# Layer norms of a float32 Perceiver-like stack: second-half squares on VectorE, later feature tiles in pairs, one set of zero products less

## What is computed

```python
def _layernorm(x, axis=-1, eps=1e-05):
    m = jnp.mean(x, axis=axis, keepdims=True)
    v = jnp.var(x, axis=axis, keepdims=True)
    return (x - m) / jnp.sqrt(v + eps)
...
x = x + _L0_xattn_ref(_layernorm(x, axis=-1), ...)
x = x + _L0_attn_ref(_layernorm(x, axis=-1), ...)
x = x + _L0_ffn_ref(_layernorm(x, axis=-1), ...)
x = x + _L1_xattn_ref(_layernorm(x, axis=-1), ...)
x = x + _L1_attn_ref(_layernorm(x, axis=-1), ...)
x = x + _L1_ffn_ref(_layernorm(x, axis=-1), ...)
```

## Time and profile before

| what | value |
|---|---|
| median of 3 runs | 1405.85 us (1403.39, 1405.93, 1405.85) |
| profiled execution, its own time | 1405.07 us |
| its span, first to last instruction | 1403.2 us |
| PE busy | 1354.3 us, 97% of the span |
| DVE, ACT, POOL busy | 983.2, 629.8, 682.5 us (70%, 45%, 49%) |
| granted TensorE clock, mean | 0.994 |
| DMA, mean | 61 GB/s |

### The profile page before, as it was taken

The page is one execution under the profiler, slowest core; times in us unless marked ns, Lnnn a source line. Parts: engine busy times, 40 slices in busy tenths (PEclk is TensorE's granted clock), DMA queues, the critical chain, the costliest instruction groups (busy, mean ns, idle before and its releaser), DMA issues.

```text
span 1403.2 us, 23741 instructions
## 1 busy us (share of the span) xinstructions
PE 1354.3 (97%) x8774; PEld 1124.2 (80%) x8774; DVE 983.2 (70%) x1501; ACT 629.8 (45%) x1325; POOL 682.5 (49%) x473
## 2 busy tenths in 40 slices
PE   6999999999999998899999999999999999999998
PEld 4677778778877776899899899999778887767886
DVE  5456676668569998787777787877546777955555
ACT  3534443253343334666566666666325545431000
POOL 3342577678737774441341331500474655626663
PEclk9999999999999999999999999999999999999999
DMA  4121123323232221000000001000132221212231
GB/s 146 49 74 47 61 84 97 90 76 95 78 141 84 87 81 60 1 26 25 1 25 24 1 25 35 19 2 1 58 107 60 76 76 61 91 38 83 91 101 63
DMA packets 30892, 85.63 MB, mean 61 GB/s; under 512 B 3408, under 2 KB 3536, under 8 KB 30544
## 3 DMA queue, kind: packets, MB, share of 16 engines
q1 hardware_dynamic: 30800, 84.43, 19.2%
HBM read 83.37 MB, written 1.05 MB: 60 GB/s over the span
## 4 chain that ended last, share of the span: by engine, by line
PE 76%; DVE 10%; ACT 7%; issue 6%; POOL 0%; DMA 0%; DVEq 0%; ACTq 0%; POOLq 0%
PE psum L904 22%; PE psum L905 21%; PE psum L906 21%; PE psum L1442 3%; DVE part_max L2596 3%; ACT expo L1981 2%; PE psum L932 1%; PE psum L940 1%; ACT expo_t L1988 1%; ACT expo L1976 1%; DVE sq_sum L2826 1%; DVE expo_t L2174 1%; DVE q_pair L2174 1%; PE psum L1635 1%; PE psum L1622 1%
## 5 line engine op out<-in xcount | busy, mean ns | idle before, releaser
L660 POOL TENSOR_SCALAR wpair<-landing 128x1024 fp32r<-128x1024 f32 (+3 forms) x116 | 108.2, 933 | 386.0 <-PE psum L906 258.7
L663 POOL TENSOR_TENSOR wpair<-landing,wpair 128x1024 fp32r<-128x1024 f32 (+3 forms) x116 | 239.3, 2063 | 9.7
L904 PE MATMUL psum<-xn,wpair 128*128 128x512 f32 (+1 forms) x552 | 212.3, 385 | 1.2 <-POOL wpair L663 0.8
L905 PE MATMUL psum<-xn,wpair 128*128 128x512 f32 (+1 forms) x552 | 208.1, 377 | 0.0
L906 PE MATMUL psum<-xn,wpair 128*128 128x512 f32 (+1 forms) x552 | 207.5, 376 | 0.0
L2174 DVE TENSOR_TENSOR expo_t<-psum,expo_t 128x512 fp32r<-128x512 f32 (+1 forms) x224 | 143.5, 651 | 76.7 <-ACT expo_t L1988 69.2
L1988 ACT CAST expo_t<-psum 128x512 fp32r<-128x512 f32 (+1 forms) x224 | 124.3, 565 | 123.8 <-PE psum L1442 123.8
L904 PE MATMUL psum<-expo_t,kv_pair 128*128 128x256 f32 (+1 forms) x416 | 133.7, 321 | 0.2 <-DVE expo_t L2174 0.2
L1442 PE MATMUL psum<-const,expo 128*128 128x128 f32 (+1 forms) x832 | 128.1, 273 | 5.3 <-DVE expo_t L2174 4.6
L2596 DVE TENSOR_REDUCE part_max<-psum 128x1 f32<-128x804 f32 x126 | 121.3, 988 | 6.1 <-PE psum L906 2.1
L761 POOL TENSOR_TENSOR wpair<-landing,wpair 128x512 fp32r<-128x512 f32 x80 | 120.9, 1511 | 6.7
(11 more groups left out here) (326 smaller groups left out, 3285.3 us busy)
## 6 DMA issues: line engine op xcount, KB each, us to landing
landing<-in_weights SPq DMA_DIRECT2D x75, 512.0 KB, 3.6
landing<-in_weights SPq DMA_DIRECT2D x105, 256.0 KB, 2.6
kv<-in_ctx SPq DMA_DIRECT2D x8, 832.0 KB, 4.4
landing<-in_weights SPq DMA_DIRECT2D x15, 320.0 KB, 2.8
rope_k<-in_rope_k SPq DMA_DIRECT2D x1, 1664.0 KB, 7.7
const<-in_constants SPq DMA_DIRECT2D x1, 1184.0 KB, 8.7
x<-in_x SPq DMA_DIRECT2D x4, 256.0 KB, 4.2
out<-x SPq DMA_DIRECT2D x1, 1024.0 KB, 4.3
```

The costliest lines, as they stand in the source:

```text
L660: pool.tensor_scalar(wpair[:, slot, 0, 0:width], landing[:, slot, 0:width], 1.0, 1.0, ALU.mult, ALU.mult).then_inc(chunk_high, 1)
L663: pool.tensor_tensor(wpair[:, slot, 1, 0:width], landing[:, slot, 0:width], wpair[:, slot, 0, 0:width].bitcast(F32), ALU.subtract).then_in ...
L904: pe.matmul(out, w(0), act(0), start=start, stop=False)
L905: pe.matmul(out, w(0), act(1), start=False, stop=False)
```

## The change

In layer norms 1 to 5 the squares of half 1 are made by DVE (`late_squares`), right behind the four subtractions, and counted on a semaphore of their own; ACT makes those of half 0 only. PE leaves out the six zero products between the two sets of square sums. In all six layer norms the normalisation works in five groups in place of eight single tiles: half 0 as tile 0, tile 1, tiles 2 and 3 together; half 1 as tiles 0 and 1 together, tiles 2 and 3 together. Product with 1/deviation, high part and low part are one instruction for a group. On ACT, Ln and Exp of half 1 now come behind the second high part instead of the fourth; on DVE, the product with 1/deviation runs two groups ahead of the low part. PE's `normal_ready` waits for the group that holds its tile.

```diff
+        NORMAL_GROUPS = ((0, 0, 1), (0, 1, 2), (0, 2, 4), (1, 0, 2), (1, 2, 4))
...
             def square_sums(k, half, pair):
 
-                pe.wait_ge(ln_squared, 4 * k + 2 * half + pair + 1)
+                if half and k:
+                    pe.wait_ge(ln_squared_late, 2 * (k - 1) + pair + 1)
+                else:
+                    pe.wait_ge(ln_squared, 2 * k + 2 * min(k, 1) + 2 * half + pair + 1)
...
                 for half in range(2):
-                    if k:
-                        keep_going(LN_BANKS[k][1 + half], 6)
+                    if k and not half:
+                        keep_going(LN_BANKS[k][1], 6)
...
             def normal_ready(k, half, f):
-                pe.wait_ge(ln_low, 8 * k + 4 * half + f + 1)
+                pe.wait_ge(ln_low, 5 * k + (((1, 2, 3, 3), (4, 4, 5, 5))[half][f]))
...
-                def high(half, f):
-                    act.wait_ge(ln_normal, 8 * k + 4 * half + f + 1)
-                    act.copy(xn[:, 0, f, HALVES[half]], xc[:, f, HALVES[half]]).then_inc(ln_high, 1)
+                def high(group):
+                    half, first, end = NORMAL_GROUPS[group]
+                    act.wait_ge(ln_normal, 5 * k + group + 1)
+                    act.copy(xn[:, 0, first:end, HALVES[half]], xc[:, first:end, HALVES[half]]).then_inc(ln_high, 1)
...
                 deviation(0)
-                squares(1, 0)
-                high(0, 0)
-                squares(1, 1)
-                for f in range(1, FT):
-                    high(0, f)
+                if not k:
+                    squares(1, 0)
+                high(0)
+                if not k:
+                    squares(1, 1)
+                high(1)
                 deviation(1)
-                for f in range(FT):
-                    high(1, f)
+                for group in (2, 3, 4):
+                    high(group)
...
-                def normalise(half):
+                def late_squares():
+                    dve.wait_ge(ln_centred, 4 * k + 4)
+                    for pair in range(2):
+                        tiles = xc[:, 2 * pair:2 * pair + 2, HALVES[1]]
+                        dve.tensor_tensor(sq[:, 2 * pair:2 * pair + 2, HALVES[1]], tiles, tiles, ALU.mult
+                                          ).then_inc(ln_squared_late, 1)
+
+                def normalise(group):
+                    half, first, end = NORMAL_GROUPS[group]
                     cols = HALVES[half]
                     dve.wait_ge(ln_rstd, 2 * k + half + 1)
-                    for f in range(FT + 1):
-                        if f < FT:
-                            dve.tensor_tensor(xc[:, f, cols], xc[:, f, cols], rstd[:, cols], ALU.mult).then_inc(ln_normal, 1)
-                        if f:
-                            dve.wait_ge(ln_high, 8 * k + 4 * half + f)
-                            low(xn[:, 1, f - 1, cols], xc[:, f - 1, cols], xn[:, 0, f - 1, cols]).then_inc(ln_low, 1)
+                    tiles = xc[:, first:end, cols]
+                    dve.tensor_tensor(tiles, tiles, rstd[:, cols].unsqueeze(1).broadcast_to([P, end - first, T // 2]),
+                                      ALU.mult).then_inc(ln_normal, 1)
+
+                def normal_low(group):
+                    half, first, end = NORMAL_GROUPS[group]
+                    dve.wait_ge(ln_high, 5 * k + group + 1)
+                    low(xn[:, 1, first:end, HALVES[half]], xc[:, first:end, HALVES[half]],
+                        xn[:, 0, first:end, HALVES[half]]).then_inc(ln_low, 1)
 
                 dve.wait_ge(ln_mean, k + 1)
                 centre(0)
                 centre(1)
+                if k:
+                    late_squares()
                 if meanwhile is not None:
                     meanwhile()
                 normalise(0)
                 normalise(1)
+                for group in range(5):
+                    normal_low(group)
+                    if group < 3:
+                        normalise(group + 2)
```

More of the change, by code:

```diff
@@ L462, in perceiver_stack @@
         ln_high, ln_low = sem("ln_high"), sem("ln_low")
+        ln_squared_late = sem("ln_squared_late")
         stored = sem("stored")
```

## The result

| | before | change |
|---|---|---|
| median of the runs taken together | 1405.89 us (6 runs, 1403.39 to 1408.46) | 1399.12 us (6 runs, 1394.86 to 1400.91) |
| ratio to before, 95% interval | | 0.9949, 0.9934 to 0.9963 |
| profiled execution, span | 1405.07, 1403.2 us | 1399.93, 1397.7 us |
| granted clock of the profiled execution | 0.994 | 0.996 |
| DVE instructions executed | 1501 | 1475 |

A second set of 10 runs of the same kernel gave 1400.59 us, just inside the range, and over all 16 the median is 1399.88.

The account below looks back on a forecast made before the run. PE was taken to bound the kernel behind each layer norm. Savings of 0.41 (layer norm 0), 0.69 (1, 3, 4) and 1.88 (2, 5) sum to 2.98 us, taking 1405.07 to 1402.1; range 1400.0 to 1404.9.

Parts of the forecast that it names:

- PE is thus 0.9 us late because ACT does the squares: Layer norm 1: first product starts at 76.83 though its low part was ready at 75.93; the change starts it 0.85 earlier.
- so they cost DVE nothing: Layer norm 1: DVE's two squares end near 73.43 and 74.03, while DVE was idle until 74.61.
- the overlap of 0.08 between DVE's instructions: Layer norms: each DVE instruction starts before the last ends; without this overlap the saving would be 1.57 us in all.
- the sums by place: Savings: 0.41 us in layer norm 0, 0.23 each in 1, 3 and 4, 0.94 each in 2 and 5.
- Here the order costs something: Layer norm 1: half 1's multiplication precedes a low part PE needs; new waits of 0.13 and 0.38, 0.62 of 0.85 lost.
- The gain does not arrive: Rival: a later meeting point, such as a PE wait for POOL, does not move; time stays near 1405; chance 0.12.
- Slower, by POOL: Rival: POOL's weight splits stretch DVE's new squares by up to 0.84 in layer norm 2; 1408 us; chance 0.04.
- DVE issues 16 instructions in place of 20 ... that is worth nothing more.: Layer norms 1 to 5: fewer DVE and ACT instructions save no further time, as both finish before PE.
- a way to be slower: Rival: PE's new layer norm gaps drop the clock to 1.2 GHz; one fall gives 1407.9, all five 1436; chance 0.03.

Follow-up runs that it names:

- before_ten_more: Kernel before with ten more DVE instructions at its start (the memset of zero_b cut into eleven pieces): median 1398.34 us, ratio 0.9952.
- change_36_more: Changed kernel with 36 more DVE instructions at its start: median 1395.98 us, ratio 0.9931 to before.
- before_ten_more_filled: Kernel before with ten more DVE instructions at its start and zero products ahead of three PE waits in stages D and E: 1397.38 us, ratio 0.9938.
- change_36_more_filled: Changed kernel with 36 more DVE instructions at its start and zero products ahead of three PE waits in stages D and E: 1391.43 us, ratio 0.9902.
- pairs_only: Changed kernel with ACT's squares of half 1 and both sets of zero products put back, tiles still in five groups: 1407.84 us, ratio 1.0020 to before.

## Why the prediction was too small, point by point

- *"PE is thus 0.9 us late because ACT does the squares"*: right. The first product is 0.75 earlier (0.85 forecast), and with squares_only, which moves the squares and drops the zero products but makes no pairs, the layer norms are as short as with the whole change.
- *"so they cost DVE nothing"*, and the overlap of 0.08 between DVE's instructions: right, as were the sums by place: 0.23 and 0.23, 0.94 against 0.87 and 0.95, 0.41 against 0.43. The rule of the Trainium skill's page "VectorE: DVE Perf Modes", section "The DRAIN you can't avoid", would have made it 1.57; the trace sides with its exception.
- *"Here the order costs something"*: right in kind, 0.23 in place of 0.38 of waiting ahead of the third tile. It costs nothing in all, since PE's first start was 0.1 later than reckoned. But the pairs also bring nothing: in layer norm 1 single tiles end at 12.25, the pairs within 0.1 of that. Their share in layer norms 1 to 5 is about zero; in layer norm 0 they are the whole of the 0.43.
- *"The gain does not arrive"*, *"Slower, by POOL"*: neither came about, and POOL's stretching was 0.27.
- **The step that failed: "DVE issues 16 instructions in place of 20 ... that is worth nothing more."** What it was worth is not the instructions' time but their number. A loop moved 18 instructions forward in DVE's stream, and at its two jumps back PE then waited 1.26 in place of 1.95 us, which is 1.4 us of waits and, by the length of stage D, 1.0 of time. The rows for it stood in the trace before (5.4 us of DVE waiting for "issue" in the stretch 660 to 830, all in two waits) and weren't read, because only the layer norms were. The Trainium skill's page "Runtime: NRT & Kernel Launch", section "Instruction fetch mechanics", says that a taken branch whose target isn't in what was fetched forces a new fetch. The idle times of 2.65 and 2.75 at the jump back, and their going with ten memsets and with some ten instruction packets fewer (28 in place of 38), agree. That the instructions had to be fetched anew is thus the likely reason, but it wasn't seen directly: the runs show that the stall hangs on how many instructions stand ahead of the loop. None of them gives a rule for its size.
- **The second step: the clock.** The sum was set against one execution at 0.994, and the clock came in only as a way to be slower, with the earlier trace rows against it. Three things were amiss. That window's 1.00 said little (in another execution of the same kernel the clock fell in layer norm 0, at 18.9, where that window ends). Outside the layer norms the clock already fell three times, for 6.8 us. And it could rise: with the shorter wait at the jump back it went from 0.9936 to 0.9957, some 2.5 us at 1.2 per 0.001. The Trainium skill's page "TensorE: Matmul & The Clock Gate", section "What's actually happening", has the clock halved after idle time; in these runs most falls, 23 of 30, stood beside a wait of PE of 1.8 to 2.4 us, but such a wait did not bring one every time, and five came with no wait at all. By that page of the Trainium skill the gaps that the change opens in the layer norms (0.60 and 0.23 us) were a reason to fear for it; the window 72 to 78 after shows 1.00:

```profile
72.00:78.00 6.00, 5.17 (x28) 3.96 (x26) 5.25 (x11) 3.62 (x9) 0.15 (x1) 1.00 0.31 87
```

In sum 2.94 (forecast 2.98) + 1.0 to 1.4 + some 2.5 from the clock make 6.4 to 6.8, against 6.2 of mean span and 6.8 of the median. The range was built from errors within the sum alone; that the first six runs fell 0.9 us out of it and the next ten 0.6 inside is the spread of the runs, and the step that failed is the same for both.

**What stays open.** At equal clock the change is worth 3.6 us with the jump back as it is, where 2.94 + 1.0 were counted; and where neither kernel has the stall, before_ten_more against change_36_more, 1.8 (filled 2.3) where 2.94 were counted. The latter gap of half a microsecond to one lies within the error of the clock correction: with the cost of its own falls taken off each trace's span, before_ten_more_filled has 1395.4 − 3.4 = 1392.0 and change_36_more_filled 1388.7, 3.3 apart. These are single executions, so it isn't settled closer than that. Why 24 fewer instructions are worse than 18 fewer, and 6 to 26 more are clean, counted in addresses, is also open.

## What to carry to other kernels

An edit that changes how many instructions an engine executes ahead of a loop can move the time by more than the edit itself: look in the waits for "issue" at each loop's jump back, before and after, and try a few dummy instructions ahead of the loop (ten here were worth 5.4 us, nearly twice the change's own 2.94). Distrust a releaser named in brackets that ended long before. And where runs of one kernel spread with the mean clock, compare at equal clock, list the waits of PE of some 2 us, and fill or shorten those (it raised the mean clock here, though not every fall stood beside one); but don't put fillers between a sum and what waits for it.

## What was unexpected of the hardware

- At DVE's jump back to the start of a loop nothing was issued for 2.04 and 2.14 us past the last thing it could have waited for (3.26 in pairs_only), sometimes with a second stall of 0.60 two instructions on; with 6 to 26 instructions more ahead of the loop, none.
- A stretch at 1.2 GHz lasted about 3.4 or 6.8 us. 23 of 30 began beside waits of PE of 1.8 to 2.4 us, five with no wait, behind 32 matmuls of 128x32. Which of the places led to one differed between executions of the same program: 6.8 and 11.9 us lost in two executions of the kernel before.
- A square on DVE that met the last 0.41 us of a POOL split took 0.96 in place of 0.69. It ended 0.69 behind 149.66, and POOL's instruction ended at 149.80. The instruction of the earlier trace rows, 1.53 in place of 0.69, ended 0.69 behind 320.90, and POOL's ended at 321.05:

```profile
319.75 1.30 POOL L761 TENSOR_TENSOR wpair<-landing,wpair 128x512 fp32r<-128x512 f32 x1
```

Both read as if DVE's instruction was held until 0.15 before POOL's ended and then ran at its own length. Two cases don't prove it.
